# Gates that travel with the scattered rows, and last gathers that add into y: a mixture-of-experts tail on one NeuronCore

## The reference

```
shared = silu(xt @ Wg_s) * (xt @ Wu_s) @ Wd_s
probs = jax.nn.sigmoid(xt @ W_router + routing_bias)
scores, idx = jax.lax.top_k(probs, TOPK)                       # 2 of 7 experts
scores = scores / jnp.sum(scores, axis=-1, keepdims=True)      # the two gates of a token
wts = jnp.sum(jax.nn.one_hot(idx, ER) * scores[..., None], axis=1)
g = jnp.einsum('th,ehi->tei', xt, Wg_r)
u = jnp.einsum('th,ehi->tei', xt, Wu_r)
combined = jnp.einsum('tei,eih,te->th', silu(g) * u, Wd_r, wts)
return (shared + combined).reshape(B, S, H)
```

## Time and profile before

| | us |
|---|---|
| median of 3 runs | 915.52 (909.67 to 917.39) |
| the profiled execution | 910.3 |
| its span, first to last instruction | 908.5 |
| the part from the first scatter to the end | 645.7 to 908.5 |
| mean granted TensorE clock | 0.968 of full speed |

### The profile page before, as it was taken

One profiled execution on the slowest core, in us unless ns is written; L12 is line 12 of the kernel. 1 busy time (PEld: TensorE's weight loads), 2 busy tenths in 40 slices (PEclk: granted clock), 3 DMA queues, 4 the chain that ended last, 5 costly groups with the idle time before them and its releaser, 6 DMA issues.

```text
span 908.5 us, 15806 instructions
## 1 busy us (share of the span) xinstructions
PE 814.3 (90%) x6028; PEld 604.5 (67%) x6051; DVE 494.2 (54%) x1057; ACT 301.5 (33%) x820; POOL 328.1 (36%) x158
## 2 busy tenths in 40 slices
PE   1799999999899998979978988799989999997982
PEld 1555455555477788968756666588868888886861
DVE  6756876669541255535764666864463434332415
ACT  2313333312532165542165656624401121111111
POOL 0000000000627333550014123343559999992050
PEclk9999999999899999999989999899999999998995
DMA  9847755564220130020196000030265543351154
GB/s 351 339 187 291 276 196 219 221 251 185 118 93 1 35 107 1 1 77 1 60 399 237 2 0 1 0 139 1 105 255 188 195 172 125 147 203 41 51 166 158
DMA packets 46697, 127.01 MB, mean 140 GB/s; under 512 B 4001, under 2 KB 8097, under 8 KB 40753
## 3 DMA queue, kind: packets, MB, share of 16 engines
q1 hardware_dynamic: 37744, 106.29, 31.3%
q10 hardware_dynamic: 6336, 11.54, 3.6%
q0 software_dynamic: 2560, 8.39, 2.8%
HBM read 102.05 MB, written 24.15 MB: 139 GB/s over the span
## 4 chain that ended last, share of the span: by engine, by line
PE 68%; DVE 8%; POOL 8%; ACT 5%; DMA 5%; issue 4%; SPq 0%; another core or an unknown queue 0%; POOLq 0%; DVEq 0%; ACTq 0%
PE scores L484 10%; PE bank L511 9%; PE bank L982 5%; PE bank L984 4%; PE bank L983 4%; DMA nat<-in_ctx_keys 3%; POOL ring_lo L1197 3%; ACT sp L1425 2%; POOL ring_hi L1195 2%; PE bank L748 2%; PE bank L646 2%; POOL x_slots L1183 2%; PE bank L559 2%; PE bank L714 2%; PE bank L561 2%
## 5 line engine op out<-in xcount | busy, mean ns | idle before, releaser
L1586 DVE STREAM_TRANSPOSE ctxT<-nat 128x1024 f32<-128x1024 f32 (+3 forms) x120 | 120.7, 1067 | 5.4 <-DMA nat<-in_ctx_keys 5.2
L484 PE MATMUL scores<-ctxT,hn 32*64 32x385 f32 (+2 forms) x2048 | 92.9, 507 | 13.2 <-DVE ctxT L1586 13.2
L511 PE MATMUL bank<-nat,probT 128*64 128x512 f32 (+1 forms) x416 | 94.2, 598 | 0.0
L1076 POOL TENSOR_TENSOR wq_lo<-wq_raw,wq_hi 128x1024 fp32r<-128x1024 f32 x4 | 9.3, 2356 | 227.1 <-ACT wq_hi L1270 227.1
L484 PEld LDWEIGHTS scores<-ctxT,hn 32*64 32x64 f32 x2048 | 64.4, 133 | 38.0 <-issue 26.8
L1197 POOL TENSOR_TENSOR ring_lo<-ring_raw,ring_hi 128x2048 fp32r<-128x2048 f32 x18 | 82.9, 4606 | 1.4
L982 PE MATMUL bank<-ring_hi,xg_lo 128*128 x176 | 73.4, 417 | 0.4 <-DVE y L2109 0.4
L984 PE MATMUL bank<-ring_hi,xg_hi 128*128 x176 | 69.5, 395 | 0.0
L983 PE MATMUL bank<-ring_lo,xg_hi 128*128 x176 | 69.0, 392 | 0.0
L1195 POOL TENSOR_TENSOR ring_hi<-ring_raw,cst 128x2048 fp32r<-128x2048 f32 x18 | 64.9, 3607 | 8.9 <-DMA ring_raw<-in_Wexp 8.9
L1124 POOL TENSOR_TENSOR sp<-sp,s_inv 128x512 f32<-128x512 f32 x16 | 16.7, 1044 | 140.3 <-DVE s_inv L1894 140.3
(11 more groups left out here) (283 smaller groups left out, 1906.3 us busy)
## 6 DMA issues: line engine op xcount, KB each, us to landing
nat<-in_ctx_keys SPq DMA_DIRECT2D x46, 1024.0 KB, 7.5
ring_raw<-in_Wexp SPq DMA_DIRECT2D x21, 1024.0 KB, 9.5
x_slots<-zeros SPq DMA_DIRECT2D x1, 5632.0 KB, 26.8
y_slots<-zeros SPq DMA_DIRECT2D x1, 5632.0 KB, 38.5
hn<-x_slots ACTq DMA_DIRECT2D x22, 256.0 KB, 3.2
y_slots<-hn ACTq DMA_DIRECT2D x22, 256.0 KB, 2.1
w_raw<-in_Wexp SPq DMA_DIRECT2D x3, 1024.0 KB, 10.0
nat<-in_ctx_keys SPq DMA_DIRECT2D x16, 130.0 KB
```

The lines of the kernel that those rows point to most:

```text
L484: last = nc.tensor.matmul(scores4[64 * b:64 * b + 64, i, 0:KEYS_IN[i]], q4[rows_i, j, 64 * b:64 * b + 64], ctxT[rows_i, b, j, 0:KEYS_IN[i] ...
L511: last = nc.tensor.matmul(bank[7][64 * b:64 * b + 64, :], probT[0:n, j, 64 * b:64 * b + 64], nat[k % 2][0:n, b, j, :], start=j == 0, stop= ...
L1586: dve.transpose(dst, src).then_inc(columns_ready, 1)
```

## The change

The rows that are scattered become 516 numbers long (`GATED = D + 4`): behind the 512 values stand the difference of the two normalised gates, the second gate, and, twice, the rank of the first pick's expert. The scatter writes 128 rows of 2064 bytes where it wrote 2048. `rows_columns_out` (DVE, for each tile) then makes a column `slot_gate` from these numbers with two small operations: where the row's first pick is this tile's expert the gate is difference plus second, else the second. ACT's copy of a tile's output takes this column as its scale. The rows in `y_slots` are so already scaled, and GpSimd's last gathers add into `y` itself (`compute_op=ALU.add`), first all eight first picks, then all eight second ones, with a wait for the first pick's landing ahead of each second pair. DVE's 16 additions are gone, and SP's stores of `y` wait for the gathers. The normalising of the gates moves from `allot` to `choose`. ACT's loads of the next tile wait for `xg_split` (DVE has read the row) instead of `xgT_full` (PE has). Some buffers move: `gated` is 16.125 KB a partition where `xx` was 16, so `wo_raw`, `xg`, `xg_lo` and `rhm_lo` get other places.

```
-        picked = [place(24 + 2 * i, f"picked{i}", [P, D]) for i in range(2 * NT)]
-        x_slots = nc.dram_tensor("x_slots", (TILES * P, D), F32).ap()
+        x_slots = nc.dram_tensor("x_slots", (TILES * P, GATED), F32).ap()
...
             for k in range(NT):
-                sp.wait_ge(y_ready, k + 1)
+                if k < NT - 2:
+                    sp.wait_ge(picked_loaded[k // 2], 4 * 16)
+                else:
+                    sp.wait_ge(picked_loaded[NT // 2 - 1], 3 * 16)
+                    if k == NT - 1:
+                        sp.wait_ge(picked_loaded[NT // 2], 16)
                 sp.dma_start(out[k * P:(k + 1) * P, :], y[:, k, :]).then_inc(stored, 16)
...
-                    nc.gpsimd.indirect_dma_start(x_slots, bass.IndirectOffsetOnAxis(slots[:, k, i:i + 1], 0), xx[:, k, :],
+                    nc.gpsimd.indirect_dma_start(x_slots, bass.IndirectOffsetOnAxis(slots[:, k, i:i + 1], 0), gated[:, k, :],
...
-            for k in range(NT):
-                for i in range(2):
-                    nc.gpsimd.indirect_dma_start(picked[2 * k + i][:], None, y_slots,
-                                                 bass.IndirectOffsetOnAxis(slots[:, k, i:i + 1], 0)).then_inc(picked_loaded[picked_part(k)[0]], 16)
+            pool.wait_ge(down_added, NT)
+            for i in range(2):
+                for k in range(NT):
+                    if i == 1 and k % 2 == 0:
+                        pool.wait_ge(pick_signal(k, 0), 2 * 16)
+                    nc.gpsimd.indirect_dma_start(y[:, k, :], None, y_slots, bass.IndirectOffsetOnAxis(slots[:, k, i:i + 1], 0),
+                                                 compute_op=ALU.add).then_inc(pick_signal(k, i), 16)
...
-                nc.scalar.copy(yo[par][:], bank[4 + par][:]).then_inc(yo_ready, 1)
+                nc.scalar.activation(yo[par][:], bank[4 + par][:], ACT.Copy, scale=slot_gate[:, ds(t, 1)]).then_inc(yo_ready, 1)
...
                 if load:
-                    act.wait_ge(xgT_full, t + 1)
+                    act.wait_ge(xg_split, t + 1)
                     load_rows(t + 2, par)
...
                     if i == 0:
+                        dve.tensor_copy(gated[:, :, D + 2:D + 4], r_key[:].unsqueeze(2).broadcast_to([P, NT, 2]))
                         chain(dve.scalar_tensor_tensor(r_p[:], r_sel[0][:], -4.0, r_p[:], ALU.mult, ALU.add))
                 dve.tensor_tensor(r_picks[:], r_sel[0][:], r_sel[1][:], ALU.add).then_inc(picks_ready, 1)
+                chain(dve.tensor_tensor(r_key[:], gates[0][:], gates[1][:], ALU.add))
+                chain(dve.reciprocal(r_key[:], r_key[:]))
+                for i in range(2):
+                    chain(dve.tensor_tensor(gates[i][:], gates[i][:], r_key[:], ALU.mult))
+                dve.tensor_tensor(gated[:, :, D], gates[0][:], gates[1][:], ALU.subtract)
+                dve.tensor_copy(gated[:, :, D + 1], gates[1][:])
...
+                dve.tensor_scalar(tile_rank[:], r_tile[:, 1, :], -1.0, float(NE + 1), ALU.mult, ALU.add)
...
-                chain(dve.tensor_tensor(r_key[:], gates[0][:], gates[1][:], ALU.add))
-                chain(dve.reciprocal(r_key[:], r_key[:]))
-                chain.mark(dve.tensor_tensor(gates[0][:], gates[0][:], r_key[:], ALU.mult))
-                dve.tensor_tensor(gates[1][:], gates[1][:], r_key[:], ALU.mult).then_inc(slots_ready, 1)
...
                 dve.wait_ge(xgT_full, t + 1)
+                dve.tensor_scalar(slot_gate[:, ds(t, 1)], xg[par][:, D + 2:D + 3], tile_rank[:, ds(t, 1)], xg[par][:, D:D + 1],
+                                  ALU.is_equal, ALU.mult).then_inc(gate_step, 1)
+                dve.wait_ge(gate_step, 2 * t + 1)
+                dve.tensor_tensor(slot_gate[:, ds(t, 1)], slot_gate[:, ds(t, 1)], xg[par][:, D + 1:D + 2], ALU.add).then_inc(gate_step, 1)
...
             hidden_split(TILES - 1)
-            for k in range(NT):
-                part, tiles = picked_part(k)
-                dve.wait_ge(picked_loaded[part], tiles * 2 * 16)
-                chain(dve.scalar_tensor_tensor(y[:, k, :], picked[2 * k][:], gates[0][:, k:k + 1], y[:, k, :], ALU.mult, ALU.add))
-                dve.scalar_tensor_tensor(y[:, k, :], picked[2 * k + 1][:], gates[1][:, k:k + 1], y[:, k, :], ALU.mult,
-                                         ALU.add).then_inc(y_ready, 1)
```

More of the change, by code:

```diff
@@ L58 @@
 RING3 = 3
+GATED = D + 4
 PLACES = [0, 2, 1, 0, 2, 1, 0]
@@ L162, in perceiver_kernel @@
         gates = [sbuf(ctx, f"gates{i}", [P, NT]) for i in range(2)]
+        slot_gate = sbuf(ctx, "slot_gate", [P, TILES])
+        tile_rank = sbuf(ctx, "tile_rank", [P, TILES])
         slots = sbuf(ctx, "slots", [P, NT, 2], U32)
         tile_expert = sbuf(ctx, "tile_expert", [P, 2, TILES], I32)
-        used_stored = sem("used_stored")
+        used_stored, gate_step = sem("used_stored"), sem("gate_step")
         expert_begins = sbuf(ctx, "expert_begins", [P, NE], I32)
@@ L242, in perceiver_kernel @@
         y_lo = place(154, "y_lo", [P, HC, P], F32R)
[L243 to L246, removed]
+        zeros = place(173, "zeros", [P, GATED])
+        gated = place(48, "gated", [P, NT, GATED])
+        xx = gated[:, :, 0:D]
+        wo_raw = place(76, "wo_raw", [P, HC, D])
+        wo_lo = place(76, "wo_lo", [P, HC, D], F32R)
         wo_hi = place(156, "wo_hi", [P, HC, D], F32R)
@@ L264, in perceiver_kernel @@
         hm = [place(172 + 2 * i, f"hm{i}", [P, HALF]) for i in range(2)]
-        r_p, r_eq, r_sel0, r_sel1 = (place(64 + i / 4, n, [P, NT, NE]) for i, n in enumerate(("r_p", "r_eq", "r_sel0", "r_sel1")))
+        r_p, r_eq, r_sel0, r_sel1 = (place(64.25 + i / 4, n, [P, NT, NE]) for i, n in enumerate(("r_p", "r_eq", "r_sel0", "r_sel1")))
         r_sel = [r_sel0, r_sel1]
[L268 to L278, removed]
+        r_key = place(65.25, "r_key", [P, NT])
+        r_picks = place(65.5, "r_picks", [P, NT, NE], BF16)
+        r_first = place(65.75, "r_first", [P, 3, NE])
+        below_bf = place(66.25, "below_bf", [P, P], BF16)
+        ones_bf = place(66.5, "ones_bf", [P, P], BF16)
+        r_begun = place(67.25, "r_begun", [P, TILES, NE])
+        r_fill = place(68.25, "r_fill", [P, NE, NE])
+        r_tile = place(68.5, "r_tile", [P, 2, TILES])
+        r_slot = place(68.75, "r_slot", [P, NT, 2])
+        r_used = place(69, "r_used", [P, TILES])
+        r_need = place(69.25, "r_need", [P, 2])
         ring_hi = place(0, "ring_hi", [P, RING3, 3, HC, D], F32R)
@@ L333, in perceiver_kernel @@
                              "rhm_split", "rhmT_ready", "rdown_full", "yo_ready"))
-        picked_loaded, y_ready = [sem(f"picked_loaded{i}") for i in range(NT // 2 + 1)], sem("y_ready")
+        picked_loaded = [sem(f"picked_loaded{i}") for i in range(NT // 2 + 1)]
         x_loaded, cst_loaded, stored = [sem(f"x_loaded{i}") for i in range(2)], sem("cst_loaded"), sem("stored")
@@ L343, in perceiver_kernel, with pick_signal @@
         dve_step = sem("dve_step")
-        def picked_part(k):
-            return (k // 2, 2) if k < NT - 2 else (k - NT // 2 + 1, 1)
+        def pick_signal(k, i):
+            return picked_loaded[NT // 2 if i == 1 and k == NT - 1 else k // 2]
         def gate_bank(j):
@@ L435, in _ @@
             sp.wait_ge(cleared, 5)
-            for rows_of in (x_slots, y_slots):
+            for rows_of, n in ((x_slots, GATED), (y_slots, D)):
                 sp.dma_start(rows_of.rearrange("(t p) d -> p t d", p=P),
-                             zeros[:].unsqueeze(1).broadcast_to([P, TILES, D])).then_inc(slots_zeroed, 16)
+                             zeros[:, 0:n].unsqueeze(1).broadcast_to([P, TILES, n])).then_inc(slots_zeroed, 16)
             for e in range(NR):
@@ L1518, in _ @@
             load_rows(1, 1)
-            act.wait_ge(xgT_full, 1)
+            act.wait_ge(xg_split, 1)
             load_rows(2, 0)
@@ L1522, in _ @@
             hidden_columns_out(0)
-            act.wait_ge(xgT_full, 2)
+            act.wait_ge(xg_split, 2)
             load_rows(3, 1)
```

9 lines of the change are left out of this document (4 added, 5 removed).

## The result

| | before | changed |
|---|---|---|
| median on the first chip, 19 runs each | 914.84 us (909.07 to 917.39) | 918.34 us (913.47 to 922.85) |
| ratio to before, 95% interval | | 1.0042, 1.0027 to 1.0058 |
| profiled execution, its span | 910.3, 908.5 | 918.3, 916.5 |
| ratio on two other chips | | 1.0134 (1.0106 to 1.0163), 1.0139 (1.0116 to 1.0162) |

The forecast was 909.4 us, the measured median 918.3: slower by 3.5 us instead of faster by 6.1. On two other chips, run later, the loss is 12 us. Before's median was lower there by ten and eleven (904.61 and 903.41), the changed kernel's by two and three (916.53 and 915.16). The ratios are estimates over all runs and can differ from the quotient of the medians by 0.1%.

The account below looks back on a forecast made before the run. PE's products and, at the expert change, GpSimd's splits bound it to 882 us, then a tail ending in DVE's additions. Without these the span ends at 902.0 + 0.4 = 902.4, -6.1; median 915.5 - 6.1 = 909.4 us, range 899.8 to 920.

Parts of the forecast that it names:

- Per tile on DVE ... Cost 0: Each tile: two one-column DVE operations, 0.4 us plus up to 0.2, covered by idle time and 2.0 us of slack.
- Were that cover gone it would be 0.6 us x 22 = 13 us: Tile loop: worst case if idle time and slack did not hide DVE's two added operations, 13 us over 22 tiles.
- The gathers add: Tail: sixteen adding gathers, 1.25 to 1.83 us apart, last packets 3.2 us after the last start, don't decide the end.
- end (b): Tail: gathers, then SP's last token-tile store; 892.4 us at period p of 1.25, reaching 902.0 only at p = 1.9.
- (a): Tail: landing of the last store to `y_slots`, at 902.0 us, forecast to decide the end.
- the longer row is cut in two: Scatters: rival, 2064-byte rows become two descriptors, scatters end 15.4 us later, +9.3 us overall; chance 0.04.
- The stall at 876 to 891: Behind the loops: ACT and DVE stand still, about 15 us; kept in the forecast, which put the next end at 902.0.
- That it closes: Behind the loops: rival, the 15 us hole disappears, span 892.8 us, -15.7, median 899.8; chance 0.17.
- The tie of the stall to the gathers: Tail: rival, the hole lasts as long as the gathers; span 911.0, median 918.0 us at period 1.83; chance 0.25.
- The router's part: Router: seven small DVE operations added to `choose`, 1.1 us, taken up by waiting; slots come at the same time, cost 0.
- The scaled copy of ACT: Each tile's output: scaling costs nothing, since silu of the same shape takes 0.60 us and the copy 0.59.
- signs named for "wrong": Changed profile: SP's stores last, DVE and ACT resuming well after 891, PE gaps in each tile, scatters over 1.3 us apart.

Follow-up runs that it names:

- Numbers 1: Changed kernel with slot_gate's one-column addition reading the gate as a per-row scalar operand instead of a second tensor; 912.67 us, ratio 1.0082 on chip B.
- number 2: Kernel before plus, in each tile, an unused one-column VectorE addition with both inputs in SBUF; 909.52 us against 905.75, ratio 1.0047 on chip B.
- numbers 9: The changed kernel without further edit, run on chip D; 915.16 us, ratio 1.0139 to the kernel before.
- 10: Changed kernel with the one-column addition's second operand as a scalar by pointer, on chip D; 912.47 us, ratio 1.0101.
- Experiment 3: Changed kernel with plain gathers and VectorE's sixteen additions back; 908.27 us, ratio 1.0026 on chip B; 909.09 us, ratio 1.0053 on chip D.
- number 5: The kernel before, unchanged, profiled once more on chip C; 900.76 us.
- 12: The kernel before, unchanged, one profiled execution on chip D; 902.88 us.
- number 7: Changed kernel with the gate added as a scalar operand, plain gathers and VectorE's sixteen additions back; 904.63 us against 904.61, ratio 0.9998 on chip C.
- 8: Changed kernel with scalar gate operand, plain gathers, VectorE's additions, and its three first-expert splits moved behind its sixth addition; 903.13 us, ratio 0.9981 on chip C.

## Why the prediction was wrong, point by point

**"Per tile on DVE ... Cost 0": the first step that failed.** The price of 0.20 us for an operation of one column came from the earlier trace rows, where all operations are in the router's part. Three facts stood in the rows and listings shown and weren't put together: the addition reads two tensors in SBUF; GpSimd is busy for 118.31 of 120 us beside it; and its splits are operations in SBUF. The slack was 2.0 us in each tile, enough for the two operations at 0.4 to 0.6 us, and the wait is up to 3.99. In the trace after, 3.5 us of lateness build up from tile 0 to tile 18 (the copies of their outputs start 6.9 and 10.4 us later than in the profile of before), and an addition of 3.38 us at 684.11 stands in tile 1's part, ahead of tile 0's multiplication. The four additions of 2.85 to 3.99 us from 712 to 799 lengthen their tiles by 0.9 to 2.0 us each, 5.6 together; those of up to 1.07 us lengthen none. At an expert's change both kernels wait for GpSimd's split (DVE for 8.02 us before, near 816, and 3.67 after, near 831), and there 1.5 us of the lateness are lost again. Numbers 1 and 2 show the mechanism, numbers 9 and 10 its price: 3.4 us. The Trainium skill (SBUF — State Buffer, Who interferes with whom) says that a VectorE instruction with two inputs in SBUF contends with a GpSimd instruction that reads SBUF, by an exclusive lock, and that issue order decides who blocks. By that rule, which speaks against this change and which I hadn't weighed, the addition waits for the end of GpSimd's operation; the trace agrees to 0.02 us, in all ten additions over 0.3 us and in the 13 of number 2.

**"Were that cover gone it would be 0.6 us x 22 = 13 us" was the wrong worst case.** The cover wasn't used up by more instructions but by one that lasts until another engine is done. In the trace after the 22 additions take 24.7 us, 1.1 each and so more than that 0.6; what reaches PE is less, since only what a single wait has beyond the slack of its tile does.

**"The gathers add": the second step that failed, and the larger.** The period was put between 1.25 and 1.83 us and measured 1.85, at the edge of the range. What was carried over unchanged was the 3.2 us from the last start to the last packet, and this is the term that was mis-sized: a gather now lands 5.9 to 7.1 us after its issue, with the DMA engines at 94 to 102%, and SP's last store is issued 7.2 us after the last gather starts. The 2.0 us of that store held (2.2; the eight stores have a median of 4.5, since the earlier ones go beside the gathers' traffic). So the step "end (b) reaches 902.0 only at p = 1.9" is wrong by its constant: from the last start to the end of the span it is 9.8 us, not 3.2 + 2.0 + 0.4 = 5.6. With the gathers starting at 868.4 as before, the end would have been 868.4 + 27.8 + 9.8 = 906.0, and (b) would have decided even so. And they don't start at 868.4: they wait for tile 18's store, which inherits all that the tiles lost. In this trace the sum is 902.4 forecast, + 3.6 (end (b) instead of (a), 906.0), + 10.5 (start at 878.88) = 916.5. Experiment 3 confirms the step: with plain gathers 7.8 us of the loss are gone on chip D. That the traffic of an adding gather is nearly double was foreseen (0.914 x 2 = 1.83, measured 1.67); that issuing it takes GpSimd 1.54 us instead of 0.949 was not.

**The 10.5 us are not all the port's.** By the trace some 3.5 us of them go with the scatters, whose last one starts that much later: this trace has three long ones,'s only one (1.97). Numbers 2, 5 and 12 show that before has the three as well in other executions; whether a scatter meets one of DVE's splits is a matter of when DVE reaches them. I had treated one execution's scatters as the kernel's. The rival "the longer row is cut in two" fell: 0.97 us each, 1280 packets.

**The stall at 876 to 891.** The prediction took the 15 us as part of the kernel, and so 902.0 as the next end. It isn't in either other execution of before that was profiled, nor in that of number 2, nor in any of the changed kernel. The one instruction packet that the prediction took as support for late code is no sign of it: it comes between 879 and 880 us in the stalled execution and in number 5's, which has no stall. That it closes was a rival, with 892.8 as the result; before itself ends at 898.9 and 901.1 without it. So the gain from dropping 11.6 us of additions had to be read from such an execution: there the additions end at about 896.5, and an adding tail from the same start ends at 906. On chip A before's median was nine to eleven us above that of the other chips and the changed kernel's two or three. All 19 executions of before there took 909.07 us or more, all 58 on the other three chips 908.96 or less. A stall in most of before's executions on chip A would explain it, but only one of them was profiled, so this is argued, not shown. What causes the stall stays open.

**A rival that came close by luck.** The tie of the stall to the gathers gave a median of 918.0 us at a period of 1.83, with a chance of 0.25, and 918.3 was measured at 1.85. Its mechanism was not there: no stall in the changed kernel, and an end set by SP's stores. That 918.3 lies inside the stated range of 899.8 to 920 is owed to the same tie, from which the upper end was built.

**What held.** The router's part, as far as can be read: the scatters began at 645.0 against 645.7, but that start lies between 641.5 and 649.8 over all profiles, so a cost of 1 us there would not be seen. The scaled copy of ACT takes 0.69 us, not 0.59 or 0.60 as estimated, hidden all the same. `slot_gate`'s two operations cost nothing that can be measured where GpSimd doesn't hold one of them (number 7), and the four waits for gathers eight ahead cost nothing. Three of the signs named for "wrong" came: SP's stores last of all, PE gaps (in some tiles, not in each), and scatters more than 1.3 us apart (three of them, which before has too).

## What to carry to other kernels

Before a small operation goes onto VectorE beside a busy GpSimd, count its inputs in SBUF: with two, an addition of one column lasted here until GpSimd's current operation ended. With a pointer scalar for the second input the same sum took 0.21 us every time. An adding gather moves work off VectorE, but it takes longer to issue, nearly twice the DMA time and longer to land; in this kernel it would have paid only with gathers that end well before VectorE does, and that needs the time of the whole tail (issue, landing, store), not the period alone. A stall that no instruction explains should be seen in a second execution before a forecast rests on it.

## What was not expected of the hardware

- A DVE addition of 128 x 1 with both inputs in SBUF took 0.16 us with GpSimd idle and up to 4.51 us beside its elementwise operations of 3.60 and 4.61 us. With the second input as a scalar by pointer: 0.212 to 0.217 us in all 22 tiles of the four kernels that have it so (numbers 1, 7, 8 and 10).
- The other way round: a scatter, 0.97 us to issue, took 2.22 to 2.84 us (1.97 once, in the first profile of before) when it started inside one of DVE's subtractions of 128 x 2048 (2.28 us, two inputs in SBUF). It ended 0.85 us after the subtraction. Moved apart, the longest was 1.16 us. DVE's additions of `y` (one input in PSUM) did not do it.
- An indirect gather of 128 rows of 2 KB that adds into SBUF: 1.54 us of GpSimd, 144 packets, 1.67 us of all 16 DMA engines, 4.7 to 7.2 us to landing over six profiles; the plain one 0.95 us, 80 packets, 0.91 us, 3.3 to 6.3 us.
